# Softplus of a fused selective-scan kernel: logarithm with the bias inside, the rounded sum by VectorE, and one more turned block per group

## The reference, cut to what matters

```python
delta = jax.nn.softplus(jnp.einsum('bkrl,kdr->bkdl', dts, dt_proj_w) + dt_proj_b[None, :, :, None])
def step(h, inp):
    d_t, u_t, B_t, C_t = inp
    h = h * jnp.exp(d_t[..., None] * A) + (d_t * u_t)[..., None] * B_t[:, :, None, :]
    return (h, jnp.einsum('bkdn,bkn->bkd', h, C_t))
```

## Time and profile before

| | |
|---|---|
| median of 3 runs | 26109.59 us (26106.97 to 26110.38) |
| the profiled execution | 26116.4 us, span 26114.6 us |
| PE busy | 24103.6 us, 92% |
| DVE busy | 24585.9 us, 94% |
| ACT busy | 22109.2 us, 85% |
| POOL busy | 20746.8 us, 79% |
| scans (L1506), 9216 | 10902.1 and 5273.0 us busy, 1804 and 1745 ns each (with a carried start value, without) |
| plain multiplications (L1501), 5600 | 5281.6 us busy, 943 ns each |

### The profile page before, as it was taken

The page is one execution under the profiler, slowest core; times in us unless marked ns, Lnnn a source line. Parts: engine busy times, 40 slices in busy tenths (PEclk is TensorE's granted clock), DMA queues, the critical chain, the costliest instruction groups (busy, mean ns, idle before and its releaser), DMA issues.

```text
span 26114.6 us, 381945 instructions
## 1 busy us (share of the span) xinstructions
PE 24103.6 (92%) x95328; PEld 13330.2 (51%) x95328; DVE 24585.9 (94%) x17625; ACT 22109.2 (85%) x50283; POOL 20746.8 (79%) x11892
## 2 busy tenths in 40 slices
PE   8999999999999999999989999999999999999998
PEld 4555555555555555555545555555555555555554
DVE  9999999999999999999989999999999999999999
ACT  8888988889888888889878888888988888988888
POOL 7777977788777977778768987778987778977778
PEclk9999999999999999999999999999999999999999
DMA  4444544444444544445444544444544444544444
GB/s 155 132 135 132 172 133 133 133 149 154 133 136 132 169 135 134 135 139 164 129 125 144 164 154 145 146 145 144 171 148 144 145 146 143 173 145 145 147 144 149
DMA packets 1419233, 3790.03 MB, mean 145 GB/s; under 512 B 205888, under 2 KB 206016, under 8 KB 1416384
## 3 DMA queue, kind: packets, MB, share of 16 engines
q1 hardware_dynamic: 1416768, 3762.72, 46.1%
HBM read 3686.39 MB, written 47.19 MB: 143 GB/s over the span
## 4 chain that ended last, share of the span: by engine, by line
PE 29%; DVE 26%; issue 25%; ACT 13%; POOL 4%; DMA 2%; DVEq 1%; SPq 0%; ACTq 0%; POOLq 0%
DVE arena L1506 11%; PE ps L813 11%; DVE ps L1501 10%; ACT arena L1246 5%; POOL arena L1646 3%; ACT arena L1180 3%; DVE arena L572 3%; PE ps L691 3%; PE ps L781 3%; PE ps L1021 2%; DMA arena<-c_rows 2%; PE ps L801 2%; PE ps L653 1%; PE ps L638 1%; PE ps L823 1%
## 5 line engine op out<-in xcount | busy, mean ns | idle before, releaser
L1646 POOL TENSOR_TENSOR arena<-arena 128x768 f32<-128x768 f32 x9216 | 16574.4, 1825 | 1406.1 <-DVE arena L1506 1090.0
L813 PE MATMUL ps<-arena,consts 128*128 128x384 f32 x36864 | 13640.4, 493 | 183.8 <-ACT arena L1280 169.7
L1506 DVE TENSOR_TENSOR_SCAN arena<-arena,carry,ps 128x768 f32<-128x768 f32 x6144 | 10902.1, 1804 | 357.3 <-PE ps L781 198.5
L1180 ACT ACTIVATE arena<-arena,An 128x768 f32<-128x768 f32 x9216 | 8458.9, 930 | 1436.1 <-POOL arena L1646 1431.0
L813 PEld LDWEIGHTS ps<-arena,consts 128*128 128x128 f32 x36864 | 6313.1, 191 | 3951.2 <-issue 486.3
L1506 DVE TENSOR_TENSOR_SCAN arena<-arena,ps 128x768 f32<-128x768 f32 x3072 | 5273.0, 1745 | 264.4 <-PE ps L781 150.3
L1501 DVE TENSOR_TENSOR ps<-ps,arena 128x768 f32<-128x768 f32 x5600 | 5281.6, 943 | 160.0 <-PE ps L801 157.0
L781 PE MATMUL ps<-consts,arena 128*128 128x128 f32 x21696 | 3055.8, 277 | 946.3 <-DVE arena L1506 750.0
L1246 ACT ACTIVATE arena<-arena 128x64 f32<-128x64 f32 (+1 forms) x13824 | 3907.9, 365 | 20.3
L1246 ACT ACTIVATE arena<-arena,bT 128x64 f32<-128x64 f32 (+1 forms) x13440 | 3813.8, 367 | 20.4
L781 PEld LDWEIGHTS ps<-consts,arena 128*128 128x128 f32 x21696 | 2482.8, 141 | 2613.2 <-issue 1425.6
(11 more groups left out here) (180 smaller groups left out, 19274.6 us busy)
## 6 DMA issues: line engine op xcount, KB each, us to landing
arena<-c_rows SPq DMA_DIRECT2D x6144, 384.0 KB, 3.8
arena<-c_rows SPq DMA_DIRECT2D x6144, 192.0 KB, 3.6
arena<-x SPq DMA_DIRECT2D x32, 864.0 KB, 7.1
arena<-arena SPq DMA_DIRECT2D x384, 72.0 KB, 2.4
arena<-mid SPq DMA_DIRECT2D x32, 864.0 KB, 6.4
c_rows<-arena SPq DMA_DIRECT2D x96, 192.0 KB, 3.1
mid<-arena SPq DMA_DIRECT2D x16, 864.0 KB, 3.9
out<-arena SPq DMA_DIRECT2D x16, 864.0 KB, 3.9
```

The lines of the kernel that those rows point to most:

```text
L813: mm = pe.matmul(y_part[:, h, :], ident, hC[it % NH][:, h * SEG:(h + 1) * SEG], start=(n == 0), stop=(n == NS - 1))
L1180: act.activation(state_at[it % NW], delta[g % 2], ACT.Exp, scale=An[:, slot(s) * NS + n:slot(s) * NS + n + 1]).then_inc(sem["da_ready"], 1)
L1506: dve.tensor_tensor_scan(a[:, ::back], a[:, ::back], slots[it % 2][:, ::back], 0.0 if k == 0 else carry[:, n:n + 1], ALU.mult, ALU.add).th ...
L1646: pool.tensor_tensor(hC[it % NH], state_at[it % NW], Csb[b], ALU.mult).then_inc(sem["hc_ready"], 1)
```

## The change

Three edits:

1. The logarithm takes the one as its bias, log(1 * e + 1), straight from e. ACT's `plus_one` (L1158) and `less_one` (L1166) go.
2. The rounded sum less one, (e + 1) - 1, is made by VectorE in one instruction with two constants (`rounded_back`), behind its scan of block 6. POOL's subtraction waits for it and, now, for the logarithm. In `first_delta`, before the scan, DVE's one combined instruction becomes this one and a subtraction.
3. `TURNED` gets one more block in every group but group 0: 8 for 7 at j = 0 and 2 (blocks 6 and 14 become plain, 5, 7 and 13 turned), 6 for 5 at j = 1 (block 4 becomes plain, 5 and 7 turned). In an image 17 blocks change from plain to turned, 544 in all.

```diff
--- before.py
+++ after.py
@@ -80,7 +80,7 @@
     return (g - g // NC) * NS + it % NS + 1 if g % NC < NC - 1 else None
 
 
-TURNED = {0: (2, 4, 6, 9, 10, 14, 15), 1: (3, 4, 9, 13, 15), 2: (2, 4, 6, 9, 10, 14, 15)}
+TURNED = {0: (2, 4, 5, 7, 9, 10, 13, 15), 1: (3, 5, 7, 9, 13, 15), 2: (2, 4, 5, 7, 9, 10, 13, 15)}
 TURNED_FIRST = (6, 10, 13, 14)
 TBL = CH // P
 
@@ -116,7 +116,7 @@
 def z_before(g):
 
     return sum(len(Z_IN.get(i, ())) for i in range(g))
-STEP_AT = dict(pre=1, taken=5, exp=5, plus=6, log=7, less=7, lost=6, log1p=7, relu=9,
+STEP_AT = dict(pre=1, taken=5, exp=5, plus=6, log=7, back=6, lost=6, log1p=7, relu=9,
                times=10, du=15, keep=1, sums=5, second=8, third=11, gate=12, turn_b=11, keep_b=13, copy_c=9)
 
 
@@ -157,7 +157,7 @@
     **{f"c_loaded{b}": 16 * NIT // NCB for b in range(NCB)},
     **{f"c_half{b}": 16 * PAIRS * NC * NS // NCB for b in range(NCB)},
     "st_hi": 2, "st_rest": 2, "st_mid": 2, "st_ready": 2,
-    "end_kept": NIT * (NC - 1) // NC, "pre_ready": NG, "pre_taken": NG, "sp_abs": 1, "sp_exp": NG, "sp_w": NG, "sp_ln": NG, "sp_rest": 1, "sp_back": NG - 1, "sp_lost": NG - 1,
+    "end_kept": NIT * (NC - 1) // NC, "pre_ready": NG, "pre_taken": NG, "sp_abs": 1, "sp_exp": NG, "sp_ln": NG, "sp_rest": 1, "sp_back": NG, "sp_lost": NG - 1,
     "sp_log1p": NG, "delta_ready": NG, "du_ready": NG,
     "b_bcast": NIT, "da_ready": NIT, "dbu_ready": plain_before(NIT), "prod_scaled": turned_before(NIT),
     "duT_full": NG, "duT_ready": NG, "bT_full": PAIRS + 1, "bT_ready": PAIRS + 1, "scanned": NIT, "hc_ready": NIT, "y_summed": NIT,
@@ -1081,7 +1081,6 @@
                 act.activation(halves(du[0]), pre_part, ACT.Abs, bias=bias).then_inc(sem["sp_abs"], 1)
                 act.wait_ge(sem["sp_abs"], v("sp_abs", 1))
                 act.activation(du[0], du[0], ACT.Exp, scale=-1.0).then_inc(sem["sp_exp"], 1)
-                plus_one(0)
                 log_part(0)
                 act.activation(halves(delta[0]), pre_part, ACT.Relu, bias=bias).then_inc(sem["pre_taken"], 1)
                 act.wait_ge(sem["c_ready"], v("c_ready", 1))
@@ -1151,19 +1150,11 @@
                 act.wait_ge(sem["pre_taken"], v("pre_taken", g + 1))
                 act.activation(e, e, ACT.Exp, scale=-1.0).then_inc(sem["sp_exp"], 1)
 
-            def plus_one(g):
+            def log_part(g):
                 if g > 0:
                     act.wait_ge(sem["sp_log1p"], v("sp_log1p", g))
                 act.wait_ge(sem["sp_exp"], v("sp_exp", g + 1))
-                act.activation(spw, du[g % 2], ACT.Identity, bias=1.0).then_inc(sem["sp_w"], 1)
-
-            def log_part(g):
-                act.wait_ge(sem["sp_w"], v("sp_w", g + 1))
-                act.activation(spln, spw, ACT.Ln).then_inc(sem["sp_ln"], 1)
-
-            def less_one(g):
-                act.wait_ge(sem["sp_ln"], v("sp_ln", g + 1))
-                act.activation(spw, spw, ACT.Identity, bias=-1.0).then_inc(sem["sp_back"], 1)
+                act.activation(spln, du[g % 2], ACT.Ln, bias=1.0).then_inc(sem["sp_ln"], 1)
 
             def scan(g):
                 s, p, j, k, c = group(g)
@@ -1198,12 +1189,8 @@
                             evacuate(g + 1)
                         if n == STEP_AT["exp"]:
                             exp_part(g + 1)
-                        if n == STEP_AT["plus"]:
-                            plus_one(g + 1)
                         if n == STEP_AT["log"]:
                             log_part(g + 1)
-                        if n == STEP_AT["less"]:
-                            less_one(g + 1)
                     if n == STEP_AT["third"]:
                         if g in Z_IN:
                             copy_z(Z_IN[g][0])
@@ -1477,12 +1464,12 @@
             def first_delta():
 
                 e = du[0]
-                dve.wait_ge(sem["sp_w"], v("sp_w", 1))
-                dve.scalar_tensor_tensor(out=e, in0=spw, scalar=-1.0, in1=e, op0=ALU.add, op1=ALU.subtract)\
-                    .then_inc(sem["sp_rest"], 1)
+                rounded_back(0)
+                dve.wait_ge(sem["sp_back"], v("sp_back", 1))
+                dve.wait_ge(sem["sp_ln"], v("sp_ln", 1))
+                dve.tensor_tensor(e, e, spw, ALU.subtract).then_inc(sem["sp_rest"], 1)
                 dve.wait_ge(sem["sp_rest"], v("sp_rest", 1))
-                dve.wait_ge(sem["sp_ln"], v("sp_ln", 1))
-                dve.tensor_tensor(e, spln, e, ALU.subtract).then_inc(sem["sp_log1p"], 1)
+                dve.tensor_tensor(e, spln, e, ALU.add).then_inc(sem["sp_log1p"], 1)
                 dve.wait_ge(sem["sp_log1p"], v("sp_log1p", 1))
                 dve.wait_ge(sem["pre_taken"], v("pre_taken", 1))
                 dve.tensor_tensor(delta[0], delta[0], e, ALU.add).then_inc(sem["delta_ready"], 1)
@@ -1505,8 +1492,17 @@
                     a = state_at[it % NW]
                     dve.tensor_tensor_scan(a[:, ::back], a[:, ::back], slots[it % 2][:, ::back],
                                            0.0 if k == 0 else carry[:, n:n + 1], ALU.mult, ALU.add).then_inc(sem["scanned"], 1)
+                    if n == STEP_AT["back"] and g + 1 < NG:
+                        rounded_back(g + 1)
                     if At.layer == 0 and n == STEP_AT["gate"] and 0 <= g - FIRST_MERGE < NC:
                         gate_merged(g - FIRST_MERGE)
+
+            def rounded_back(g):
+
+                if g > 1:
+                    dve.wait_ge(sem["sp_lost"], v("sp_lost", g - 1))
+                dve.wait_ge(sem["sp_exp"], v("sp_exp", g + 1))
+                dve.tensor_scalar(spw, du[g % 2], 1.0, -1.0, ALU.add, ALU.add).then_inc(sem["sp_back"], 1)
 
             def gate_sums():
 
@@ -1661,7 +1657,8 @@
 
             def rounded_off(g):
                 e = du[g % 2]
-                pool.wait_ge(sem["sp_back"], v("sp_back", g))
+                pool.wait_ge(sem["sp_back"], v("sp_back", g + 1))
+                pool.wait_ge(sem["sp_ln"], v("sp_ln", g + 1))
                 pool.tensor_tensor(e, e, spw, ALU.subtract).then_inc(sem["sp_lost"], 1)
 
             def log1p(g):
```

## The result

The changed kernel takes 26168.5 us (median of 14 runs, 26154.5 to 26179.9), the kernel before 26109.7 us on the same chip. The ratio is 1.0023, 95% interval 1.0015 to 1.0030: +58.8 us, a little more than this kernel's measurement can tell from no change. The forecast was 26150 in a range of 26010 to 26280; its limit for "slower" was 26162, and the time lies 7 us beyond it.

A forecast was written before the change was run, and what follows sets the result against it. DVE sets the pace, but ACT, PE and POOL are nearly full too. Group terms of +35 us and +10 ahead of them took 26116 to 26161, less 7 for the median, rounded to 26150; range 26010 to 26280, own range 26080 to 26200.

The forecast's parts named there:

- No gain from DVE's relief: Whole kernel: DVE's net 240 us less work would not shorten the time, since other engines lack room; +45 us.
- The first rival: Whole kernel: DVE stays the bound and the 240 us come through, 25880 us, or 26000 with half; chance 0.18.
- The cost of the new instruction: DVE, behind scan 6: the rounded-sum instruction takes 0.55 us, 544 times, 299 us in all.
- POOL's floor in groups 10 to 14: POOL needs 35.8 us a group, so groups 10, 11, 13, 14 give only -0.4 us; 6 and 12 +0.5.
- Late rows for block 7: ACT's scaling delays slot 7, by 1.4 us in group 3; groups 1 and 3 grow 1.0 us each.
- PE's waits for rows: Whole span: PE's waits for scaled rows rise from 191 to some 1000 us.
- The third rival: After scan 6, DVE's instruction waits for POOL's product, 0.9 us on average: 490 us, 26640; a quarter, 26270; chance 0.05.
- Groups 7 to 9, 15 and 17: Per image: groups 7 to 9 +0.7 us (PE's merge), 15 and 16 +0.6 (PE full), 17 -1.0 (no new instruction).
- The sum: Group terms of +1.1 us an image, times 32, +35 us, plus +10 us ahead of the groups: +45 us.

The follow-up runs named there:

- The table alone: The kernel before with only the new table of turned blocks, ACT still making the plus-one and less-one: +371.9 us against the kernel before (ratio 1.0144).
- the run on one column: The changed kernel with DVE's new instruction on 1 column instead of 768, rounding correction left out: -13.7 us against the kernel before, 72 us below the changed kernel.
- Cutting POOL's work: The changed kernel with POOL's four instructions of the step on 64 columns instead of 768: -153.6 us against the kernel before, 212 below the changed kernel.
- fitted lists: The changed kernel with a list of turned blocks for each of the 17 groups, fitted to the new step: 25959.6 us, -153.2 against the kernel before.
- halves: The kernel before with the new table alone: +371.9 us; the changed kernel with the table of before: +192.0 us, both against the kernel before.
- a list for each group: The kernel before, step on ACT, with a list of turned blocks for each of the 17 groups: 25879.3 us, ratio 0.9911 to the kernel before.
- the run with lists: The changed kernel with a list of turned blocks for each group and DVE's new instruction on 1 column: 25804.4 us, -306.7 against the kernel before.

## Why the prediction was right or wrong

- **No gain from DVE's relief: right, and shown.** The table alone costs 372 us although DVE works 449 us less. The first rival is out for the whole; it holds in groups 2 and 5, as the run on one column shows. DVE's busy time fell by 183 us, not 240.
- **The cost of the new instruction: right in kind, 0.08 us too high.** 0.55 was taken, 0.47 is measured from start to start in the groups where nothing delays it (2.18 - 1.71), 0.53 as a record.
- **POOL's floor in groups 10 to 14: right in cause, wrong in what it leaves.** I gave these four -0.4 us together and +0.5 to groups 6 and 12. Measured in groups 10, 11, 13 and 14 is 0.0, +0.1, +0.1 and +0.1; group 12 grew by 0.25, group 6 by 0.1 in the second layer, and by 1.1 in the first, where `gates` and not POOL's floor sets it. (By the prediction's own floor, 35.8 against 35.6 or 35.7, groups 6 and 12 would have got 0.3 together, not 0.5.) Cutting POOL's work brings groups 10 to 14 down to DVE's own sum. What the prediction lacked are the ways from POOL to DVE: through the state buffers and ACT's queue to the slot of block 5 (groups 13 and 14), through PE's sum to the first slot of the next group (groups 12 to 14), and in groups 10 and 11 the slot of block 13, a turned one now, behind PE's four sums. Group 10 of the fourth image in the changed kernel, DVE and PE:

```profile
3028.54 1.81 DVE L1493 TENSOR_TENSOR_SCAN arena<-arena,carry,ps 128x768 f32<-128x768 f32 x1 [0.41 <-PE ps L781]
...
3025.10 0.81 PE L818 MATMUL ps<-arena,consts 128*128 128x384 f32 x2
...
3027.68 0.82 PE L781 MATMUL ps<-consts,arena 128*128 128x128 f32 x6
```

The sums take PE from 3025.10 to 3027.68, the slot is full at 3028.5, and the scan waits 0.41 us for it. From scan 12 to scan 13 it takes 2.22 us here and 1.83 with POOL's work cut, so 0.4 of this comes from POOL as well.
- **Late rows for block 7: the size right, the cause only in part.** Groups 1 and 3 grew by 1.06 and about 1.0 us, as written, and the sum hits by this. In group 3 the step holds for the larger part: slot 7 is filled 1.6 us later in the mean (1.4 was given), DVE does not wait for it, but slot 13 comes 1.0 later. Leaving out most of that scaling gives back 0.4 and 0.9 us of the 0.8 and 1.2 by which group 3 grew in the two layers. In group 1 it gives back nothing. There it is PE's gapless stretch with the rows of C, which begins later because block 4 became plain. I had reckoned with the block that was turned, and not with the one that was turned back. In group 3 POOL's lateness counts too (0.9 and 1.1 us less without its step's work); which share each has stays open, since the trials overlap.
- **PE's waits for rows: far too high.** I wrote 1000 us; they are 421. The table alone, without ACT's relief, has 933.
- **The third rival, DVE waiting for POOL: it did not decide, but it exists.** It is real where POOL runs late: group 3, with records up to 2.15 us; 28 us in all, where the rival had 490. In the changed kernel it hides there (the run on one column left group 3 within 0.04 us in the second layer and made it 0.6 longer in the first); with fitted lists the instruction and its wait cost 1.2 to 1.3 in group 3.
- **Groups 7 to 9, 15 and 17:** smaller shifts than given. Group 17 gained its 1.0 us in the first layer alone; in the second it stayed at 38.2 us, with the table alone too. PE holds it there: at block 8, in the second layer alone, its queue has eight further matmuls (L1021), and it works without a gap from there to slot 9. In image 20 they begin 15.44 us into the group in both kernels, so what DVE gains ahead of them is waited away at scan 9, which starts 20.56 us into the group in both:

```profile
16559.07 2.94 PE L1021 MATMUL ps<-arena,consts 128*128 128x384 f32 x8
...
16564.19 3.76 DVE L1493 TENSOR_TENSOR_SCAN arena<-arena,carry,ps 128x768 f32<-128x768 f32 x2 [1.10 <-PE ps L781]
```

- **The sum:** 45 us predicted, 47 in the span, 59 by the medians. It rests on errors of up to 21 us of both signs by groups, and on group 6 of the first layer, whose 17 us it did not see; that it came so near is luck in part. The prediction's own range is 10 us off as well: -1 to +2.5 us an image are 26080 to 26190, not 26200.

The exclusion of DVE and POOL, for which the Trainium skill (SBUF — State Buffer, section Who interferes with whom) has a rule, agrees with the traces both ways: 2.04 us for POOL's product beside the instruction, 0.69 to 1.95 for the instruction beside a product.

## What to carry to other kernels

Where four engines are each within some 3 us of a 36 us group, a relief of one is worth what the others can use, so test the halves of a change by themselves: here they cost 372 and 192 us, and together 59. When a table trades one kind of block for another, look at both the block that is added to the slow side and the one that goes back, against the fixed work in each queue; a list for each group gave 0.9% without any new instruction. And before work is moved to a DVE instruction that excludes POOL, ask where POOL has a product in flight: the same instruction took 0.53, 0.70 or 1.95 us by place.

## What the runs showed of the hardware

- An instruction of 1 column was never held up by POOL: it took 0.13 us in all 544 places, though in 70 of them a product of POOL was running (in the run with lists in 311), while the one of 768 columns took up to 2.15 us and one of 18 columns elsewhere 0.72.
- DVE's TENSOR_SCALAR of 768 columns with two constants took 534 ns, the one of the earlier trace rows, whose scalar comes by partition, 613. The latter also reads its source in rows of 48 out of a wider image, so which of the two makes the difference is not shown.
